# A state-space and cross-attention kernel on one core: the static places of its jobs in four engine orders are drawn anew

## The reference, cut to what matters

```python
p = silu(prepend_cond @ pre_w1) @ pre_w2
h = concatenate([p, x], axis=1)
for l in range(4):                       # mamba_block(rmsnorm(h)) is added to h
    xi, z = split(xn @ ip_w)             # 512 channels each
    xi = silu(causal_conv4(xi) + cb)     # four taps
    dt, Bm, Cm = split(xi @ xp_w)        # 16, 16, 16
    dt = softplus(dt @ dtp_w + dtp_b)
    # for each channel e and each of 16 states s, over time:
    #   h[e,s] = exp(dt*A) * h[e,s] + dt*Bm[s]*xi ;  y[e] = sum_s h[e,s]*Cm[s]
    y = (y + xi * D) * silu(z)
    h = h + y @ op_w
x = rmsnorm(h)[:, 64:]
x = x + softmax(q k^T) v @ Wproj + bproj   # q, k, v of layernorms, 16 heads
x = x + gelu(layernorm(x) @ W1 + b1) @ W2 + b2
```

## Time and profile before

| what | us |
|---|---|
| median of 3 runs (lowest, highest) | 8656.73 (8644.46, 8657.88) |
| the profiled execution, its own time | 8651.71 |
| its span | 8649.6 |
| PE, DVE, POOL, ACT busy | 7703.4, 6773.9, 6305.4, 5602.4 |
| a prefix step (start of scan 0 to the next) | 114.50 |
| a main step | 99.70 |
| from the first `up` of the pieces with jobs to the first scan of the next block | 157.90 |

### The profile page before, as it was taken

One profiled execution on the slowest core, in us unless ns is written; L12 is line 12 of the kernel. 1 busy time (PEld: TensorE's weight loads), 2 busy tenths in 40 slices (PEclk: granted clock), 3 DMA queues, 4 the chain that ended last, 5 costly groups with the idle time before them and its releaser, 6 DMA issues. The chain is left out here.

```text
span 8649.6 us, 202213 instructions
## 1 busy us (share of the span) xinstructions
PE 7703.4 (89%) x86784; PEld 5260.7 (61%) x86784; DVE 6773.9 (78%) x6490; ACT 5602.4 (65%) x8563; POOL 6305.4 (73%) x3428
## 2 busy tenths in 40 slices
...
GB/s 63 43 45 58 44 52 46 60 44 47 44 46 25 35 61 49 47 44 47 44 46 25 50 52 44 47 44 47 53 42 20 55 47 44 47 44 57 53 38 10
DMA packets 133307, 391.15 MB, mean 45 GB/s; under 512 B 49581, under 2 KB 78189, under 8 KB 95553
## 3 DMA queue, kind: packets, MB, share of 16 engines
...
## 5 line engine op out<-in xcount | busy, mean ns | idle before, releaser
L1197 DVE TENSOR_TENSOR_SCAN arena<-arena,ps 128x512 f32<-128x512 f32 x4608 | 5594.1, 1258 | 642.0 <-issue 477.1
L1422 POOL TENSOR_TENSOR arena<-arena 128x1024 f32<-128x1024 f32 x2240 | 5275.4, 2365 | 846.8 <-DVE arena L1197 817.8
L560 PEld LDWEIGHTS ps<-arena 64*128 64x128 f32 x36864 | 2331.8, 191 | 1594.0 <-DVE arena L1197 894.5
L882 ACT ACTIVATE arena<-arena,rate 128x512 f32<-128x512 f32 (+1 forms) x4608 | 3042.5, 713 | 340.0 <-DVE arena L1197 314.3
L560 PE MATMUL ps<-arena 64*128 64x128 f32 x36864 | 2766.0, 289 | 394.3 <-DVE arena L1197 373.2
L579 PE MATMUL ps<-csts,arena 64*128 64x64 f32 x35840 | 1517.9, 224 | 28.5 <-POOL arena L1422 28.1
L579 PEld LDWEIGHTS ps<-csts,arena 64*128 64x128 f32 x35840 | 1435.8, 140 | 40.6 <-POOL arena L1422 34.0
L615 PE MATMUL ps<-arena 128*128 128x512 f32 x1152 | 674.7, 678 | 189.9 <-DVE arena L1227 170.7
L1443 POOL TENSOR_TENSOR arena<-arena 128x512 f32<-128x512 f32 x288 | 371.0, 1288 | 601.7 <-ACT arena L1022 501.0
L1227 DVE SCALAR_TENSOR_TENSOR ps<-arena,ps 128x512 f32<-128x512 f32 x576 | 428.6, 744 | 347.8 <-ACT ps L969 346.5
L1431 POOL TENSOR_TENSOR arena<-csts,arena 128x512 f32<-128x512 f32 x576 | 606.4, 1055 | 83.6 <-ACT arena L1007 83.6
(11 more groups left out here) (109 smaller groups left out, 6439.1 us busy)
## 6 DMA issues: line engine op xcount, KB each, us to landing
...
```

What stands on the lines that cost most here:

```text
L560: i = nc.tensor.matmul(o, dtxT[half[h], c, b, :], diagB[half[h], pair, b, :].rearrange("p (i s) -> p i s", s=Q), start=True, stop=True)
L882: nc.scalar.activation(o, i, ACT.Exp, scale=rate[:, ph.layer(n), g:g + 1]).then_inc(decay.sem, 1)
L1197: nc.vector.tensor_tensor_scan(hs[:, place(n, v) + g % 2, :], dA[:, g % RING, :], pair[:, g % Q::Q], init[:, n % 2, g:g + 1] if ph.main() ...
L1422: nc.gpsimd.tensor_tensor(hs[:, a:a + 2, :], hs[:, a:a + 2, :], Crep[:, 2 * pair:2 * pair + 2, :], ALU.mult).then_inc(prod.sem, 1)
```

## The change

The tables of places get new numbers. No instruction of the computation is added or removed, and the sizes stay; seven of the 25 jobs change their bank in the prefix and one (`z1`) in the main steps. The rule by which the 64 units lie between the feed-forward pieces, before by formulas, is now a list of ends. A line or two of each table:

```diff
-PRE_PE = {0: [("dxT1", 0), ("out0.0", -1)], 1: [("out0.1", -1)], 2: [("out0.2", -1)], 4: [("yt3", -1)],
+PRE_PE = {1: [("dxT1", 0), ("out0.1", -1)], 2: [("out0.2", -1)], 3: [("yt3", -1)], 5: [("out0.3", -1), ("out1.0", -1)],
...
-          26: [("dt1", 1)], 28: [("yt2", 0)], 30: [("dxT0", 1)]}
+          23: [("dt2", 1)], 24: [("dt3", 1), ("dt0", 1)], 25: [("dt1", 1)], 27: [("yt2", 0)], 29: [("dxT0", 1)],
+          30: [("out0.0", 0)]}
...
-PRE_POOL = {2: [("dtx2", 0)], 9: [("dtx3", 0)], 28: [("dtx0", 1)], 31: [("dtx1", 1)]}
+PRE_POOL = {2: [("dtx2", 0)], 10: [("dtx3", 0)], 27: [("dtx0", 1)], 30: [("dtx1", 1)]}
...
-           29: [("out1.3", -1)], 30: [("dxT2", 1), ("z0.0", 2)], 31: [("z0.1", 2)]}
+           30: [("dxT2", 1), ("z0.0", 2), ("z0.1", 2)], 31: [("z1.0", 2)]}
...
-            10: [("dt2", 1)], 11: [("dt3", 1)], 12: [("dt0", 1)], 13: [("dt1", 1), ("soft", 1), ("rstd", 2)],
+            12: [("dt0", 1), ("skip3", 0)], 13: [("dt1", 1), ("rstd", 2)], 14: [("soft", 1)], 19: [("xi0", 2)],
...
-MAIN_DVE = {13: [("gate2", -1)], 15: [("gate3", -1)], 34: [("norm0", 2)], 35: [("norm1", 2)], 37: [("res0", -1)],
+MAIN_DVE = {13: [("gate2", -1)], 16: [("gate3", -1)], 31: [("norm0", 2)], 35: [("norm1", 2)], 37: [("res0", -1)],
...
-NEXT_AT = {("up", 1, 7): range(0, 26)}
-NEXT_AT.update({("up", 2, f): range(26 + f, 27 + f) for f in range(8)})
...
+NEXT_ENDS = [14, 18, 20, 23, 23, 23, 26, 26, 28, 29, 31, 32, 35, 35, 38, 41, 41, 42, 42, 42, 43, 45, 47, 50, 53, 56, 58, 59]
+NEXT_ITEMS = MLP_ORDER[MLP_ORDER.index(("up", 1, 7)):]
+NEXT_AT = {j: range(a, b) for j, a, b in zip(NEXT_ITEMS, [0] + NEXT_ENDS, NEXT_ENDS + [64])}
-MAIN_POOL = {0: [("dtx3", 0)], 16: [("dtx0", 1)], 22: [("dtx1", 1)], 26: [("dtx2", 1)]}
+MAIN_POOL = {3: [("dtx3", 0)], 15: [("dtx0", 1)], 22: [("dtx1", 1)], 25: [("dtx2", 1)]}
```

More of the change, by code:

```diff
@@ L43 @@
 PRE_BANK = {"out0": 1, "yt3": 0, "out1": 0, "dxT1": 0, "ms": 1, "dxT2": 0, "xi0": 0, "xi1": 1, "dxT3": 0, "xi2": 0,
-            "xi3": 1, "z0": 0, "z1": 1, "z2": 0, "z3": 1, "yt0": 0, "xp": 1, "yt1": 0, "bT": 1, "dt2": 1, "dt3": 0,
-            "dt0": 1, "dt1": 0, "yt2": 0, "dxT0": 1}
-MAIN_BANK = {"z0": 0, "z1": 1, "z2": 0, "z3": 1, "yt2": 0, "yt3": 1, "xp": 0, "dxT3": 1, "bT": 0, "ms": 1, "dt0": 0,
+            "xi3": 1, "z0": 0, "z1": 0, "z2": 1, "z3": 1, "yt0": 0, "xp": 1, "yt1": 0, "bT": 1, "dt2": 0, "dt3": 0,
+            "dt0": 0, "dt1": 1, "yt2": 1, "dxT0": 0}
+MAIN_BANK = {"z0": 0, "z1": 0, "z2": 0, "z3": 1, "yt2": 0, "yt3": 1, "xp": 0, "dxT3": 1, "bT": 0, "ms": 1, "dt0": 0,
              "dt1": 0, "dt2": 0, "dt3": 0, "out0": 0, "xi0": 1, "yt0": 0, "dxT0": 0, "xi1": 1, "yt1": 0, "xi2": 1,
```

17 lines of the change are left out of this document (6 added, 11 removed), and 46 rows, old and new, of tables (MAIN_ACT, MAIN_DVE, MAIN_PE, PRE_ACT).

## The result

The changed kernel takes 8271.67 us (median of 4 runs, 8270.90 to 8273.25) against 8652.09 for the kernel before (4 runs, 8644.46 to 8657.88): ratio 0.9561, 95% interval 0.9544 to 0.9578, a gain of 380 us where 245 were forecast.

A forecast was written before the change was run, and what follows sets the result against it. Main steps were taken as bound by the order of things, with neither PE nor DVE full. Gains of 129 (main), 42 (prefix) and 74 (block seams) sum to 245 off 8651.7: 8407, forecast as 8412 for the median, range 8350 to 8552.

The forecast's parts named there:

- the main steps' sum: Main steps: 1.05 + 0.65 + 0.55 = 2.25 us a step, giving a step of 97.5 and -129 us in all.
- step 6: Main step's last group: xi3.1 in unit 27 instead of 28 ends the 1.22 us wait at g58, counted as 0.55.
- Step 1: Main step's start: z1.0 to unit 31 of the step before, z0.1 to 30, shortening PE's stretch by 1.05 us.
- Steps 2 to 4: Main step: rstd ahead of soft ends g34's 1.12 us wait; norm0 at g31 hidden by 0.4; moved skips cost about 0.3.
- steps 2 to 5: Main step: root, norm0, skip and y0, xi0 and gate0 moves together bring 0.65 us beyond the z part's 1.05.
- Step 5: Main step: xi0 ahead of y1, gate0 ahead of tap00; tap00's 0.84 us wait goes, gate0 waits about 1 us.
- The prefix: Six seams between prefix steps: half of the waits at g0 and g4 goes, 7 us a seam, -42 us (0 to -89).
- The block seams: Three seams between blocks: respaced up pieces cover xi waits, less wait behind the load; 24.5 us each, -74 us.
- Only PE's part pays: Rival: in main steps waits for PE replace the three ACT waits; -107 us in all, 8550; chance 0.13.
- A table switch costs more than its row: Rival: main step's added table load ahead of g36 costs another 1.28 us, 77 us given back, 8489; chance 0.09.
- Slower through norm0: Rival: norm0 at g31 of main steps holds DVE until Exp; at 6 us later, 90 us slower, 8747; chance 0.06.
- all three upper bounds: Largest gains allowed: 180 us for main steps, 89 for the prefix, 32 for each of three block seams.

The follow-up runs named there:

- the four edits together: Kernel before with z parts moved, root ahead of Softplus and norm0 at g31, y1 in unit 20 and gate0 at g39, xi3 whole in unit 27: 8488.13 us.

## Why the prediction was right and wrong

**The failed step is the main steps' sum: 2.25 us a step were forecast and 4.5 came.** The kind of mechanism was right: a step gets shorter where a moved job ends a wait. What failed is which places were counted, and at what price. Three things make up the miss: the residual's move from g61 to g60 was no term at all (1.20 a step), step 6 was put at 0.55 and gave 1.3 to 1.4, and the steps that lost time at a lower clock were no term (0.57 a step). These overlap in part. In one sum, the four edits together gave 2.97 a step against the 2.25, res1 1.20 and dxT0 0.18: 4.35 of the 4.52 that all main tables gave. Even the 180 us that the prediction had as the most for these steps lie far below the measured 254.

- *Step 1, z parts, 1.05.* It gave half: 24 us alone and 23 undone, 0.54 and 0.57 a step. Alone, the wait moves to g0 because z0 waits there for the residual. I had put 0.4 of wait there but in no term.
- *Steps 2 to 4, root, norm0, skips.* The root and norm0 gave 46 us alone and 30 undone (0.65 a step, with a shift to gate0). The order was as described, norm0 at g31 waits for nothing, and g36 waits 0.38 instead of 0.1. I had 0.65 for steps 2 to 5 together, which this edit fills by itself.
- *Step 5, xi0 ahead of y1, gate0 ahead of tap00.* The two together give 43 alone. In the changed kernel the evictions' order, which I had as the reason, gives nothing; in the kernel before it was not run apart from gate0's place. What I did not see is that gate0 frees the bank for dxT0, which the change has a unit earlier: with gate0 back, the kernel is 188 slower.
- *Step 6, xi3.1, 0.55.* It gave 68 us alone and 71 undone, 1.41 and 1.34 a step: all of the 1.22 of the earlier trace rows and a little more. I took half off because PE would be later at g58 and g0, and no wait came there.
- *No term at all: res1 from g61 to g60.* It gave 68 us. I had shown PE's wait of 1.02 for it and spent it as slack for the z part. In fact it stood ahead of the input of g0, so the edit that ends it is a term of its own.
- *No term at all: the clock.* In the kernel before, 16 of the 52 steps have a granted clock of 1.00, and they take 99.74 where the mean is 100.31. In the changed kernel all 52 have 1.00. The difference of 0.57 is 34 us over 60 steps. It is part of what the edits above gave and comes on top of none of them.
- *PE's share as a limit.* I took 92.7 busy as work, and with the stalls shorter it is 91.0. Single steps at a granted clock of 1.00 have 91.85 before and 90.91 after, so about half of the fall is the clock and the other half is not explained. PE's idle time came out at 4.8 as forecast, but by luck: both the step and the busy time are shorter than I had them.

**The prefix: 42 forecast, 59 by the stamps, 49 undone.** The waits at g0 and g4 went in full. The new wait is 7.3 and not 3, and at g58 and not g62. The forecast had dxT0 and POOL for it; the rows show y2's eviction behind Softplus on ACT, at which the forecast looked only for the number of table loads. That moving y2 ahead of Softplus would end it is argued from the rows and was not run. The size came near in part by luck: half of two waits, 7 a seam, was a round choice, and the other waits that came and went were not in it.

**The block seams: 74 forecast, 71 by the stamps, 68 undone.** This was right in size and in mechanism: 131.6 against about 133, one wait of 2.29 left of the three (2.2 forecast), xi at 1.9, the granted clock at 0.96, and 39.2 against 38.5 for the part behind the load. One reading was wrong without harm: all of xi2, and not half of it, stood behind the one up piece.

**The range.** Its low end was said to be two thirds of the way to the upper bounds, but 150 and 65 lie less far than that; two thirds would give about 163, 73 and 89, and 8332. The measured 8271.67 lies below that as well, and below the 8292 of all three upper bounds together.

**The rivals.** *Only PE's part pays*: no. xi3, the root and gate0's edit, which end waits for ACT, gave 68, 46 and 43 us alone, against 24 for PE's z part. *A table switch costs more than its row*: no. The first activation starts 0.02 after the load and g36 waits 0.38 and not 1.4. The Trainium skill (ScalarE: Activation LUTs, What ACT_TABLE_LOAD costs) has 1380 ns of drain for a switch; these rows do not show it. *Slower through norm0*: no, norm0 has no wait.
